# A Mamba-2 layer's state-space part as one program by blocks of 512 tokens, with the value convolution as tap-scaled products

## The reference

```
u      = x * rsqrt(mean(x*x) + 1e-6) * norm_w              # x: layer norm of the part before
z, xBC, dt = split(u @ in_proj_w.T)                        # 256, 512 and 4 columns
xBC    = silu(sum over k of conv_w[:, k] * xBC[t - 3 + k] + conv_b)   # four taps, causal
x, B, C = split(xBC)                                       # 256 (4 heads of 64), 128, 128
dt     = softplus(dt + dt_bias);  dA = exp(-exp(A_log) * dt)
h      = h * dA + dt * B outer x                           # state: 4 heads x 64 x 128
y      = h . C + D * x
out    = y * silu(z)                                       # goes to the mixer's tail
```

## Time and profile before

| | us |
|---|---|
| median of three runs | 1882.82 (1882.42 to 1883.24) |
| the profiled execution | 1885.1 |
| its span, first to last instruction | 1883.3 |
| PE busy in the span | 1666.7 |
| DVE busy | 1335.5 |
| ACT busy | 1141.9 |
| POOL busy | 200.9 |
| mean granted TensorE clock | 0.929 |

### The profile page before, as it was taken

One profiled execution on the slowest core, in us unless ns is written; L12 is line 12 of the kernel. 1 busy time (PEld: TensorE's weight loads), 2 busy tenths in 40 slices (PEclk: granted clock), 3 DMA queues, 4 the chain that ended last, 5 costly groups with the idle time before them and its releaser, 6 DMA issues. The chain is left out here.

```text
span 1883.3 us, 25598 instructions
## 1 busy us (share of the span) xinstructions
PE 1666.7 (88%) x9916; PEld 795.1 (42%) x9916; DVE 1335.5 (71%) x1849; ACT 1141.9 (61%) x2305; POOL 200.9 (11%) x160
## 2 busy tenths in 40 slices
PE   6699999999999998857999999999794376699998
PEld 4233333333333333343444444455562344344443
DVE  4988888888888886258788677674474676355654
ACT  5078888888888887741677877777444511333432
POOL 1000000000000100110010001111522041100100
PEclk9699999999999999967899999999897777799999
DMA  2000000000000000010000000000000000100000
GB/s 94 0 1 1 1 1 1 1 1 1 1 1 1 1 1 1 1 45 0 1 1 1 1 1 1 2 1 2 1 1 0 0 1 27 61 1 6 6 1 12
DMA packets 4665, 13.32 MB, mean 7 GB/s; under 512 B 344, under 2 KB 2400, under 8 KB 4192
## 3 DMA queue, kind: packets, MB, share of 16 engines
q1 hardware_dynamic: 4544, 11.68, 1.9%
HBM read 10.63 MB, written 1.05 MB: 6 GB/s over the span
## 5 line engine op out<-in xcount | busy, mean ns | idle before, releaser
L636 DVE TENSOR_REDUCE a_part_max<-a_ps 128x2 f32<-128x1024 f32 x512 | 602.1, 1221 | 85.2 <-PE a_ps L495 84.4
L621 ACT ACTIVATE a_probs<-a_ps 128x512 f32<-128x512 f32 x1024 | 532.7, 615 | 128.7 <-PE a_ps L553 126.4
L636 DVE TENSOR_REDUCE f_part_max<-f_ps 128x2 f32<-128x1024 f32 (+3 forms) x320 | 327.3, 1061 | 121.6 <-PE f_ps L495 65.3
L553 PE MATMUL a_ps<-a_q_shift,a_KA 64*128 64x512 f32 x1024 | 366.0, 446 | 3.9 <-POOL a_q_shift L476 2.7
L621 ACT ACTIVATE f_probs<-f_ps 128x512 f32<-128x512 f32 (+3 forms) x640 | 300.3, 538 | 99.1 <-PE f_ps L553 48.6
L495 PE MATMUL a_ps<-a_KA,a_q_open 64*128 64x512 f32 x1024 | 285.0, 484 | 14.5 <-DVE a_part_max L636 13.8
L553 PEld LDWEIGHTS a_ps<-a_q_shift,a_KA 64*128 64x128 f32 x1024 | 166.9, 186 | 289.0 <-ACT a_probs L621 274.0
L571 PE MATMUL a_psO<-a_probs,a_VA 128*32 128x512 f32 x2048 | 274.6, 608 | 3.9 <-ACT a_probs L621 3.9
L553 PE MATMUL f_ps<-f_q_shift,f_KA 64*128 64x512 f32 (+3 forms) x640 | 222.9, 434 | 4.8 <-ACT f_probs L621 2.2
L495 PE MATMUL f_ps<-f_KA,f_q_open 64*128 64x512 f32 (+3 forms) x640 | 175.2, 452 | 17.0 <-DVE f_part_max L636 16.2
L553 PEld LDWEIGHTS f_ps<-f_q_shift,f_KA 64*128 64x128 f32 x640 | 106.6, 188 | 148.9 <-ACT f_probs L621 138.9
(11 more groups left out here) (311 smaller groups left out, 1765.2 us busy)
## 6 DMA issues: line engine op xcount, KB each, us to landing
experts_w<-in_experts SPq DMA_DIRECT2D x1, 3264.0 KB, 12.6
W<-in_weights SPq DMA_DIRECT2D x1, 2086.0 KB, 10.5
out<-X SPq DMA_DIRECT2D x4, 256.0 KB, 2.3
select<-in_select SPq DMA_DIRECT2D x1, 768.0 KB, 13.9
K<-in_consts SPq DMA_DIRECT2D x1, 644.0 KB, 7.0
R<-in_rows SPq DMA_DIRECT2D x1, 530.0 KB, 6.1
X<-in_x SPq DMA_DIRECT2D x1, 0.5 KB, 6.4
C<-in_cols SPq DMA_DIRECT2D x1, 15.0 KB, 5.3
```

The lines of the kernel that those rows point to most:

```text
L553: mm = pe.matmul(bank(r)[:, lo:512], g.KA[rows, 2 * n + jp, P * s:P * s + P], q_shift[rows, u % 2, jp, lo:512], start=True, stop=not diag)
L621: nc.scalar.activation(probs[:, st % 2, j, lo:512], bank(r)[:, lo:512], ACT.Exp, scale=SCALE).then_inc(ring_read, 1)
L636: dve.tensor_reduce(part_max[:, 4 * q + 2 * jp:4 * q + 2 * jp + 2, c], ps1[:, k % 2, :, 0:b - a], AX_X, ALU.max).then_inc(max_read, 1)
```

## The change

**In the expert stage.** Beside the norm `X` of each block, the scaled input of the state-space part is made there: POOL computes `u_scale` from the variance by five operations on four columns, DVE a second `minus_mean`, ACT a second `apply_norm` into `U`, PE transposes `U` (`turn_u`) and ACT copies it with `norm_w` into `UT`, a tile with three zero columns ahead of the 2048 tokens. For blocks 0 and 1 the transposes and copies are in the lists of blocks 2 and 3, for the last two blocks at the end. The tiles `OT`, `X1` and `Y` of that part are allocated in another order and place.

**One stage for the rest.** `rms_transposed`, `ssm_in_stage` and `ssm_stage` are replaced by `state_space_stage`. It produces the inputs of block `n+1` while the recurrence runs over the four chunks of block `n`. `dt` is computed at the start for all tokens. The nine items of a block that go through PSUM (two projections, two convolved halves of `x`, transposes and gates) share a ring of two banks: PE's `slot` waits until the item two before has been read (`ring_read`). For the values `x`, the four taps are no longer applied on DVE: POOL multiplies `in_proj_w` by each tap once (`taps`), and PE sums four products of `UT`, shifted by one column each (`convolve`); ACT's Silu adds the bias. `B` and `C` keep their convolution on DVE, by blocks of 512. `a` is spread over the triangle by ACT (`spread_a`), four activations of 128 columns per chunk, rather than by POOL. `D*x` is made by ACT (`skips`) and added by PE as an identity product in `outputs`. `z` is multiplied in by chunk (`finish`). `weigh`, `carry_on` and `finish` are the chunk's DVE work; `values` and `decayed` make `xd` and `xs` by block, and `values(n, 0)` stands after `weigh` and `carry_on` of the block's last chunk.

```diff
+                def turn_u(b):
+                    pe.wait_ge(u_done, 4 * b + 4)
+                    if b:
+                        pe.wait_ge(ut_sb, b)
+                    else:
+                        pe.wait_ge(ct_sb, NB)
+                    for i in range(4):
+                        mm = pe.transpose(ps[:, 6, P * i:P * i + P], U[:, b % 2, i, :], g.k("ident"))
+                    mm.then_inc(ut_ps, 1)
...
+                    if i == 2 and b >= 2:
+                        turn_u(b - 2)
...
+                turn_u(NB - 2)
+                turn_u(NB - 1)
...
+                    pool.wait_ge(rstd3, b + 1)
+                    pool.tensor_tensor(ms[:, b, :], mv[:, 2, b, :, 1], rstd[:, 2, b, :], ALU.mult).then_inc(ms_step, 1)
+                    pool.wait_ge(ms_step, 4 * b + 1)
+                    pool.tensor_tensor(ms[:, b, :], ms[:, b, :], rstd[:, 2, b, :], ALU.mult).then_inc(ms_step, 1)
+                    pool.wait_ge(ms_step, 4 * b + 2)
+                    pool.tensor_scalar(ms[:, b, :], ms[:, b, :], 1e-6, None, ALU.add).then_inc(ms_step, 1)
+                    pool.wait_ge(ms_step, 4 * b + 3)
+                    pool.tensor_tensor(ms[:, b, :], ms[:, b, :], half4, ALU.pow).then_inc(ms_step, 1)
+                    pool.wait_ge(ms_step, 4 * b + 4)
+                    pool.tensor_tensor(u_scale[:, b, :], ms[:, b, :], rstd[:, 2, b, :], ALU.mult).then_inc(u_scaled, 1)
...
+                    act.wait_ge(u_mean, b + 1)
+                    if b >= 2:
+                        act.wait_ge(ut_ps, b - 1)
+                    apply_norm(nc, U[:, b % 2], blk(g.Y, b), u_scale[:, b, :], u_nb[:, b, :], u_done)
+                def copy_ut(b):
+                    act.wait_ge(ut_ps, b + 1)
+                    at = CONV - 1 + 512 * b
+                    nc.scalar.activation(g.UT[:, at:at + 512], ps[:, 6, :], ACT.Identity, scale=g.c("mnorm")).then_inc(ut_sb, 1)
...
+                        if i == 3 and b >= 2:
+                            copy_ut(b - 2)
...
+                    dve.wait_ge(u_scaled, b + 1)
+                    minus_mean(dve, mv[:, 2, b], u_scale[:, b, :], u_nb[:, b, :], u_mean)
...
+    ITEMS, COPY_B, COPY_C, X0, X1, T_X0, Z0, T_X1, Z1, T_B = 9, 0, 1, 2, 3, 4, 5, 6, 7, 8
...
+                sp.dma_start(rows[:], g.aps["conv_rows"].rearrange("(k c) -> k c", k=CONV).partition_broadcast(P))\
+                    .then_inc(rows_in, 16)
...
+                pool.wait_ge(rows_in, 16)
+                pool.tensor_tensor(taps[:], rows[:], g.w("mxbc")[:, 0:DI].unsqueeze(1).to_broadcast([P, CONV, DI]),
+                                   ALU.mult).then_inc(taps_in, 1)
...
+                def slot(n, item):
+                    k = ITEMS * n + item
+                    if k >= 2:
+                        pe.wait_ge(ring_read, k - 1)
+                    return ring(k)
...
+                def convolve(n, x):
+                    bank = slot(n, X0 + x)
+                    if n == 0 and x == 0:
+                        pe.wait_ge(taps_in, 1)
+                    for k in range(CONV):
+                        mm = pe.matmul(bank, taps[:, k, P * x:P * x + P], g.UT[:, 512 * n + k:512 * n + k + 512],
+                                       start=(k == 0), stop=(k == CONV - 1))
+                    mm.then_inc(ring_ps, 1)
...
+                def decays_of(c):
+                    pe.wait_ge(al_done, MH * (c + 1))
+                    if c >= 2:
+                        pe.wait_ge(exp_done, c - 1)
+                    pe.matmul(d_bank(c), g.k("after"), al[:, c % 4].rearrange("p h i -> p (h i)"),
+                              start=True, stop=True).then_inc(d_ps, 1)
...
+                def outputs(c):
+                    n, i = c // 4, c % 4
+                    if c >= 2:
+                        pe.wait_ge(y_out, c - 1)
+                    pe.wait_ge(ring_read, ITEMS * n + T_X1 + 1)
+                    pe.matmul(y_bank(c)[:, 0:DI], g.k("ident"), skip[:, n % 2, i, :], start=True, stop=False)
+                    pe.wait_ge(w_done, c + 1)
+                    pe.wait_ge(xd_done, 2 * n + 2)
+                    for h in range(MH):
+                        pe.matmul(y_bank(c)[:, HD * h:HD * h + HD], seg[:, c % 8, h, :],
+                                  xd[:, n % 2, i, HD * h:HD * h + HD], start=False, stop=(h == MH - 1))
+                    if c:
+                        pe.wait_ge(state_done, c)
+                    else:
+                        pe.wait_ge(cleared, 1)
+                    pe.matmul(y_bank(c)[:, DI:2 * DI], xbc[:, n % 2, 3, P * i:P * i + P], states[:, c % 4, :],
+                              start=True, stop=True).then_inc(y_ps, 1)
...
+                pe.wait_ge(a_done, 1)
...
+                turn_x(0, 0)
+                gate(0, 0)
+                turn_x(0, 1)
+                gate(0, 1)
+                turn_b(0)
+                for c in range(4):
+                    decays_of(c)
+                scores(0)
+                for b in range(NB):
+                    n = b + 1
+                    for i in range(4):
+                        c = 4 * b + i
+                        if n < NB and i == 0:
+                            project(n, COPY_B)
+                            project(n, COPY_C)
+                        if n < NB and i == 1:
+                            convolve(n, 0)
+                        if n < NB and i == 2:
+                            convolve(n, 1)
+                            turn_x(n, 0)
+                        if n < NB and i == 3:
+                            gate(n, 0)
+                            turn_x(n, 1)
+                            gate(n, 1)
+                            turn_b(n)
+                        if i < 3:
+                            scores(c + 1)
+                        outputs(c)
+                        if n < NB and i == 3:
+                            for k in range(4):
+                                decays_of(4 * n + k)
+                            scores(4 * n)
...
+                def skips(n, x):
+                    k = ITEMS * n + (T_X0, T_X1)[x]
+                    act.wait_ge(xd_done, 2 * n + x + 1)
+                    if n >= 2:
+                        act.wait_ge(y_ps, 4 * (n - 2) + 4)
+                    for h in range(2):
+                        src = ring(k).rearrange("p (t c) -> p t c", c=P)[:, :, HD * h:HD * h + HD]
+                        at = 2 * x + h
+                        ins = nc.scalar.activation(skip[:, n % 2, :, HD * at:HD * at + HD], src, ACT.Copy,
+                                                   scale=g.r("dskip")[:, at:at + 1])
+                    ins.then_inc(ring_read, 1)
...
+                def spread_a(c):
+                    if c >= 4:
+                        act.wait_ge(d_ps, c - 3)
+                    for h in range(MH):
+                        nc.scalar.activation(al[:, c % 4, h, :], g.k("upto"), ACT.Copy,
+                                             scale=a[:, c, h:h + 1]).then_inc(al_done, 1)
+                def exponent(c):
+                    act.wait_ge(d_ps, c + 1)
+                    if c >= 8:
+                        act.wait_ge(y_ps, c - 7)
+                    nc.scalar.activation(seg[:, c % 8].rearrange("p h i -> p (h i)"), d_bank(c), ACT.Exp).then_inc(exp_done, 1)
...
+                silu_conv(0, 0)
+                silu_conv(0, 1)
+                silu_taps(0, 0)
+                silu_taps(0, 1)
+                for c in range(2):
+                    spread_a(c)
+                skips(0, 0)
+                silu_z(0, 0)
+                skips(0, 1)
+                silu_z(0, 1)
+                copy_b(0)
+                for c in range(2, 4):
+                    spread_a(c)
+                for c in range(4):
+                    exponent(c)
...
+                for b in range(NB - 1):
+                    n = b + 1
+                    copy_pad(n, 0)
+                    copy_pad(n, 1)
+                    for c in range(4 * n, 4 * n + 4):
+                        spread_a(c)
+                    silu_conv(n, 0)
+                    silu_conv(n, 1)
+                    silu_taps(n, 0)
+                    silu_taps(n, 1)
+                    skips(n, 0)
+                    silu_z(n, 0)
+                    skips(n, 1)
+                    silu_z(n, 1)
+                    copy_b(n)
+                    for c in range(4 * n, 4 * n + 4):
+                        exponent(c)
...
+                def weigh(c):
+                    dve.wait_ge(sc_ps, c + 1)
+                    if c >= 2:
+                        dve.wait_ge(w_done, c - 1)
+                    dve.tensor_tensor(gm[:, c % 2], s_bank(c)[:, 0:P], g.k("upto"), ALU.mult).then_inc(gm_done, 1)
+                    dve.wait_ge(gm_done, c + 1)
+                    dve.wait_ge(exp_done, c + 1)
+                    dve.tensor_tensor(seg[:, c % 8], seg[:, c % 8], gm[:, c % 2].unsqueeze(1).to_broadcast([P, MH, P]),
+                                      ALU.mult).then_inc(w_done, 1)
...
```

(34 more changed lines are left out.)

486 lines of the change are left out of this document (209 added, 277 removed).

## The result

The changed kernel takes 1861.76 us (median of 4 runs, 1860.77 to 1863.02) beside 1883.03 for the kernel before (4 runs, 1882.42 to 1883.9): ratio 0.9887, 95% interval 0.987 to 0.9904, 21.3 us faster. The forecast was 1863, range 1845 to 1880.

A forecast was written before the change was run, and what follows sets the result against it. No engine was full in the replaced stretch; the recurrence was bound by the DVE-PE chain. Start 1441.5 plus 38+81.3+14.6+2 = 136 put the tail 18.7 earlier, with -1 about -20: 1865, median 2.3 lower, 1863; range 1845 to 1880.

The forecast's parts named there:

- End of the expert stage, +9.3: Added scale work delays the new program's start: 3.8 ScalarE, 1.4 GpSimd queue, 4.1 after the last power; bounds +5 to +15.
- The 3.8 for ScalarE: Expert stage's end: ScalarE's added scale work in blocks 2 and 3 makes the last expert product 3.8 us later.
- Scaling, −12.4: Old scaling before the first projection (square, reduction, power, scaling, transposes, copies) vanishes, 12.4 us.
- Prologue, 38: From the new program's start to the scores of chunk 0: 38 us.
- A block, 27.1: Each of three blocks producing the next one's inputs: 27.1 us, bound by PE's 25.8 plus waits of 0.7 and 0.6.
- rival 1: The block's end is serial: PE waits 5 us per block, not 1.3, and 3 more in the prologue; 1877, chance 0.2.
- Last block, 14.6: Recurrence without further production, DVE bound: 3.3 us per chunk, 13.2, and a last finish; 14.6 us.
- Low level in the first block, +2, and −1 for the tail: Some first-block products still at TensorE's low level, +2 us; tail's first transposes after less PE idling, -1 us.
- Rival 2: Better: expert-stage work hides, taps arrive at 9, prologue at full level, blocks without waits; 13.7 us more, 1849, chance 0.15.
- Rival 3: TensorE falls to low level in the blocks; their 77 us of products take 77/L at mean level L; slower, chance 0.1.
- Rival 4: No change: the serial block end and the small GpSimd operations' +15 together, 1882; chance 0.03.
- the 1870 that the page's figure gave: Silu and Exp table switches at about 2.7 us each, not 1.28, add about 7 us: 1870.

The follow-up runs named there:

- after_again: The changed kernel measured once more with no edit; 1861.36 us, ratio 0.9885 to the kernel before.
- e1: The changed kernel with three of the four tap products of each value half left out; 1859.37 us, ratio 0.987.
- e11: As e1, one tap product of four, with five idle 512-column products per block where TensorE stood waiting; 1857.87 us, ratio 0.9859.
- e2: The changed kernel with the values' convolution put back on VectorE, without the four tap products; 1878.01 us, ratio 0.9969.
- e5: The changed kernel with VectorE making the next block's values before weighing this block's last chunk; 1858.31 us, ratio 0.9866.
- e12: The changed kernel with the edits of e3 and e5, plus idle products as in e6 and five in the prologue; 1848.41 us, ratio 0.9816.
- e4: The kernel before the change with only the spreads of a moved from GpSimd to ScalarE; 1873.32 us, ratio 0.9946.
- e3: The changed kernel with the spreads of a moved back from ScalarE to GpSimd; 1854.85 us, ratio 0.9844.
- e7: The changed kernel with the B and C projections placed before the 32 dt products; 1862.28 us, ratio 0.9888.
- e6: The changed kernel with ten and five idle 512-column products before the expert stage's last two token turns; 1855.08 us, ratio 0.9847.

## Why the prediction was right, and where it was not

- *The total.* 1863 for 1861.76 is in part luck. By the traces the forecast was 19.7 us less (18.7 before the tail and 1 in it), and measured were 24.3, nearly all before the tail. The start was 1.3 too late in the sum, the first block's low level 2 and the last block 1.4 too long. That the medians differ by 21.3 only, and so come near the forecast, is owed to where the two profiled executions lie beside their medians.
- *End of the expert stage, +9.3.* Program start 1440.15, 7.95 later than the scaling's start (forecast 1441.5). From the last expert product it is 16.87 us before and 22.24 after, +5.4 where 1.4+4.1 was forecast. The small GpSimd operations take 0.20 (0.3 taken), the power 1.04, the chain 2.2 (2.5). Block 3's power comes at 1424.41, 1.1 later against the last expert product than before (1.4). The 3.8 for ScalarE was 2.6 by the two traces, within the spread that `after_again` shows, so its size is not settled. The whole term was 1.3 too high.
- *Scaling, −12.4.* Gone.
- *Prologue, 38.* Scores at 1478.1, 38.0 after the start, but by errors that cancel. The dt products took 6.96 and not 5.6: PE stayed at 0.50 through 6.8 busy us. The rows arrived in 3.8 us and the `taps` product took 2.34 (6.1 and 3.9 forecast), so the tap products began at 10.0 all the same, behind PE's own work and not behind the taps. The price of `spread_a`, 0.28 read from PSUM input, was 0.30 in a row (2.42 for eight). The ring wait is there, 2.20. GpSimd's price of 1.94 per 512 columns was misread: it is a mean over 16 products, of which the first four took 17.08 us together, most of it beside VectorE's passes over 4096 columns, and the other twelve 1.04 to 1.32 each. The second trace of the same kernel has 1.8 more: a term good to some 2 us.
- *A block, 27.1.* Measured 26.9 with the two waits at 0.75 and 0.70 (0.7 and 0.6). PE is right (25.4 of 25.8). VectorE's tap was mis-sized: 2.35/4 scaled to 0.62, measured 0.752, and 0.78 with its hand-over. What failed is the sentence "so PE binds, and the value convolution is why". The block is VectorE's unbroken 16.3 us and the 10.6 us of steps behind it: e1 and e11 took 5.2 us of tap products away and it did not get shorter, e2 made VectorE's stretch longer and it grew by the same 5.65, e5 made it shorter and it fell until TensorE's own 25.4 us held it. The two bounds are 1.5 us apart. The number came out because the two waits were in the forecast, as VectorE's order and near their size; that they belong to a chain that sets the period, whatever TensorE's sum, was not. That is what rival 1 describes, at the small price that the forecast gave it.
- *Last block, 14.6.* 13.2 to the tail's first instruction: 2.97 per chunk where 3.3 was taken.
- *Low level in the first block, +2, and −1 for the tail.* Neither came. Blocks are at 1.00 from the start; the tail's projection took 3.78 us in both profiles of the changed kernel, and less in some others (2.05 to 3.72) without an edit there.
- *The rivals.* Rival 1 as a time (1877) did not happen. Rival 2 did not happen; that e12 is at its 1849 is by other means. Rival 3, the low level in the blocks, did not happen after. It did in e1 (0.88) and e2 (0.79), where TensorE had waits of 1 to 3 us in each block, but at a smaller price than 77/L: 0.5 us of a block in e1 and none in the block of e2 that is shown, because the slower products filled time in which TensorE would have waited. Rival 4 no.
- *The table loads.* Ten in the new program, 1283 ns each; six are in the blocks. There the first exponential still waited 0.73 us for a decay product after the load had ended, and after the load for the silus and the first of them ScalarE waited 4.43 us for the tap products, so neither load cost the block anything; the first silu began 0.02 us after its load. The Trainium skill, ScalarE: Activation LUTs, Rules for kernel authors, budgets about 2.7 us per switch; the trace disagrees in size, and the 1870 that the page's figure gave is 8 us above the result.
- *The order of the gains.* In the old program the spreads off GpSimd are worth 10 us alone (e4); in the new one the tap products are worth 16 (e2), by the VectorE work that they replace, and ScalarE as the place of the spreads costs 7 (e3).

## What to carry to other kernels

When an engine is busy 94% of a steady block, look once more at what its last waits are. Here VectorE, busy 72% of the block, was the bound: its work stood in one unbroken stretch, and the steps behind it had to end before the next could begin. Freeing the busy engine then bought nothing, and its lower clock was mostly a consequence of the waits, not the cause of the time. The test is to measure the other engine's longest stretch without a pause, and to see whether it and the block change by the same amount. A move of work that pays in one schedule has to be priced again in the new one; here the same move, the spreads from GpSimd to ScalarE, is worth −10 us and +7. Compare single traces by distances inside them: up to 4 us of the ends were no edit's.

## What was unexpected of the hardware

- 32 products of 4 columns took 6.83 to 6.96 us in all twelve traces of the new program, at a granted clock of 0.50 from the first to the last, with TensorE and its weight load both busy nearly without a gap. With two products of 512 columns ahead of them (e7) TensorE was busy throughout 1438 to 1449 us and still at 0.50.
- In e6 the granted clock went from 1.00 to 0.50 over a barrier at which TensorE stood idle for 2.28 us.
- GpSimd's product of 512 columns depends on what VectorE does: the first four of the old recurrence took 17.08 us together, most of it beside VectorE's passes over 4096 columns, the other twelve 1.04 to 1.32 us each; in e3 it took 5.61/4 = 1.40 beside VectorE's convolution and 4.03/4 = 1.01 at the blocks' ends, where VectorE was mostly idle. VectorE pays too: its product with `seg` took 1.21 us in the eight chunks of the old recurrence in which a GpSimd product ran beside it, and 0.69 in seven others; without GpSimd (e4) the mean is 693 ns.
